# Attention sums on one core: accumulating transfers for every second tile, visits two stretches behind the scores

## The reference, cut to what matters

```python
q, k, v = x @ wq, x @ wk, x @ wv          # 32, 8 and 8 heads of 32
scores = einsum('bihd,bjhd->bhij', q, k) * 32 ** -0.5   # causal
attn = softmax(scores, axis=-1)
out = einsum('bhij,bjhd->bihd', attn, v).reshape(b, s, 1024) @ wo
```

## Time and profile before

| | us |
|---|---|
| median of 3 runs (3458.98 to 3460.59) | 3460.47 |
| the profiled execution | 3461.34 |
| its span in the trace | 3459.6 |
| PE busy | 3405.6 (98%) |
| POOL busy | 1747.4 (51%) |
| DVE busy | 2002.3 (58%) |
| ACT busy | 1467.6 (42%) |

### The profile page before, as it was taken

The page is one execution under the profiler, slowest core; times in us unless marked ns, Lnnn a source line. Parts: engine busy times, 40 slices in busy tenths (PEclk is TensorE's granted clock), DMA queues, the critical chain, the costliest instruction groups (busy, mean ns, idle before and its releaser), DMA issues.

```text
span 3459.6 us, 61790 instructions
## 1 busy us (share of the span) xinstructions
PE 3405.6 (98%) x25202; PEld 2389.0 (69%) x25202; DVE 2002.3 (58%) x3617; ACT 1467.6 (42%) x1830; POOL 1747.4 (51%) x749
## 2 busy tenths in 40 slices
PE   8999999999999999999999999999999999999998
PEld 7888886565665665666666566556558888878887
DVE  3122116777677677677777767767746766642222
ACT  3111112555665565565565556556553223211111
POOL 0000003888988998898898898889540000000000
PEclk9999999999999999999999999999999999999999
DMA  6334344021111111211112111110037777655553
GB/s 217 112 125 124 114 135 97 22 55 50 32 46 50 38 38 50 51 30 48 50 33 53 50 35 43 50 40 10 26 113 239 232 234 229 220 203 167 170 174 132
DMA packets 248556, 340.60 MB, mean 98 GB/s; under 512 B 55648, under 2 KB 150368, under 8 KB 248288
## 3 DMA queue, kind: packets, MB, share of 16 engines
q1 hardware_dynamic: 248288, 336.87, 32.6%
HBM read 203.08 MB, written 133.17 MB: 97 GB/s over the span
## 4 chain that ended last, share of the span: by engine, by line
PE 77%; POOL 18%; ACT 2%; DVE 2%; issue 1%; DMA 0%; POOLq 0%; ACTq 0%; SPq 0%; DVEq 0%
POOL p_psums L694 16%; PE p_acc L42 13%; PE p_o L771 12%; PE p_acc L44 12%; PE p_acc L43 12%; PE p_qm L722 11%; PE p_km L764 8%; PE p_km L757 2%; DVE p_part_max L883 1%; POOL p_psums L690 1%; ACT p_probs L847 1%; PE p_ag_ps L1198 1%; PE p_qm L726 1%; PE p_km L759 1%; PE p_acc L1187 1%
## 5 line engine op out<-in xcount | busy, mean ns | idle before, releaser
L883 DVE TENSOR_REDUCE p_part_max<-p_qm 128x1 f32<-128x512 f32 (+3 forms) x2240 | 1400.7, 672 | 556.0 <-PE p_qm L722 348.4
L694 POOL TENSOR_TENSOR p_psums<-p_psums,p_probs 128x1024 f32<-128x1024 f32 x620 | 1480.3, 2388 | 92.5 <-ACT p_probs L847 2.9
L847 ACT ACTIVATE p_probs<-p_km 128x1024 f32<-128x1024 f32 x896 | 887.6, 1023 | 463.1 <-PE p_km L764 451.7
L722 PE MATMUL p_qm<-p_k_st,p_q_st 96*128 96x512 f32 (+3 forms) x2560 | 907.8, 415 | 10.3 <-ACT p_neg_max L829 4.5
L722 PEld LDWEIGHTS p_qm<-p_k_st,p_q_st 96*128 96x128 f32 x2560 | 473.9, 191 | 255.7 <-issue 93.2
L764 PE MATMUL p_km<-p_q_st,p_k_st 97*128 97x512 f32 x1792 | 602.8, 418 | 12.6 <-ACT p_probs L847 8.3
L771 PE MATMUL p_o<-p_probs,p_v 128*32 128x256 f32 (+1 forms) x9216 | 566.6, 372 | 0.0
L771 PEld LDWEIGHTS p_o<-p_probs,p_v 128*32 128x32 f32 x9216 | 271.1, 110 | 222.1 <-issue 52.3
L764 PEld LDWEIGHTS p_km<-p_q_st,p_k_st 97*128 97x128 f32 x1792 | 311.3, 192 | 101.2 <-ACT p_probs L847 59.9
L690 POOL TENSOR_TENSOR p_psums<-p_probs 128x1024 f32<-128x1024 f32 x110 | 261.9, 2381 | 189.2 <-ACT p_probs L847 189.2
L679 POOL MEMSET p_k_st<- 1x2048 f32 x2 | 3.6, 1805 | 511.6 <-PE p_acc L44 511.6
(11 more groups left out here) (153 smaller groups left out, 3980.9 us busy)
## 6 DMA issues: line engine op xcount, KB each, us to landing
p_q_st<-q_hi SPq DMA_DIRECT2D x128, 256.0 KB, 4.7
p_x_raw<-in_xT SPq DMA_DIRECT2D x64, 256.0 KB, 3.5
q_hi<-p_out_hi SPq DMA_DIRECT2D x64, 256.0 KB, 2.0
q_lo<-p_out_lo SPq DMA_DIRECT2D x64, 256.0 KB, 2.4
p_q_st<-q_lo SPq DMA_DIRECT2D x64, 256.0 KB, 4.4
attended_T<-p_o_raw SPq DMA_DIRECT2D x128, 128.0 KB
p_a_raw<-attended_T SPq DMA_DIRECT2D x32, 512.0 KB, 9.7
p_recip<-reciprocals SPq DMA_DIRECT2D x128, 128.0 KB, 6.9
```

Of the source, the lines that this page charges most:

```text
L694: pool.tensor_tensor(sums[:, :, :], sums[:, :, :], probs[(n * NS + s) % PB][:, :, :], ALU.add).then_inc(added, 1)
L722: last = pe.matmul(bank[:, x * keys:(x + 1) * keys], q_st[par][0:ROWS, c, h + x, sub * P:(sub + 1) * P], k_st[par][0:ROWS, j * CK:j * CK + ...
L847: act.activation(tile[:, :, :].rearrange("p h q -> p (h q)"), km[s % 2][:, :, :].rearrange("p a b -> p (a b)"), ACT.Exp, scale=SCALE).then ...
L883: dve.reduce_max(part_max[c][:, h:h + heads, sub, j], qm[bank_of(i)][:, 0:item_width(i)].rearrange("p (h k) -> p h k", h=heads), AX.X).the ...
```

## The change

The plan now gives each chunk a written order of work for its sums. Chunks 4 to 7 have a chain of tiles 4, 6, 8, 10 (2, 3, 4 and 4 of them) that POOL doesn't add itself. SP copies the first of the chain (tile 4) to a new buffer `fsums` (512 KB; there is one), and POOL then issues, for each further tile of the chain, a transfer inside SBUF that adds the tile to `fsums` (`accum_op`). Each of these waits for the landing of the one before. At the end of the chunk POOL waits for the last landing and adds `fsums` to its own sum. The plan:

| chunk | 0 | 1 | 2 | 3 | 4 | 5 | 6 | 7 | all |
|---|---|---|---|---|---|---|---|---|---|
| tiles | 2 | 4 | 6 | 8 | 10 | 12 | 14 | 16 | 72 |
| to POOL before | 0 | 3 | 5 | 6 | 8 | 9 | 11 | 12 | 54 |
| to POOL after | 0 | 3 | 5 | 6 | 7 | 7 | 8 | 10 | 46 |
| to the transfers after | 0 | 0 | 0 | 0 | 2 | 3 | 4 | 4 | 13 |
| adds of POOL before | 0 | 2 | 4 | 5 | 7 | 8 | 10 | 11 | 47 |
| adds of POOL after (the combining one counted) | 0 | 2 | 4 | 5 | 7 | 7 | 8 | 10 | 43 |

POOL's order in chunk 7, for example, is: adds of tiles 1, 2, 3, 5, transfer of 6, add of 7, transfer of 8, add of 9, transfer of 10, adds of 11, 12, 13, the combining add. The last group has its plan of before. The ring has 21 tiles instead of 22 (`fsums` takes the place of one). PE visits a stretch two stretches behind its scores instead of one (`LAG`), so the last two stretches of a group are visited in the next group, and stores and the load of v move with them. The diff, cut to its core:

```diff
-    PB = 22
+    PB = 21
+    LAG = 2
...
-    POOLED = [0, 3, 5, 6, 8, 9, 11, 12]
-    SUMS = Sums(POOLED)
-    LAST_SUMS = Sums([c + 1 if c > 2 else 0 for c in range(NC)])
+    def order(fetched, added):
+        if not added:
+            return []
+        chain = [4 + 2 * x for x in range(fetched)]
+        tiles = [t for t in range(NT) if t not in chain][:added]
+        steps = []
+        for t in sorted(chain + tiles):
+            if t in chain:
+                steps.append(("fetch" if t > chain[0] else "copy", t))
+            else:
+                steps.append(("add" if steps else "first", t))
+        if fetched:
+            steps.append(("fetched", 0))
+        return steps
+    SUMS = Sums([order(*counts) for counts in ((0, 0), (0, 3), (0, 5), (0, 6), (2, 7), (3, 7), (4, 8), (4, 10))])
+    LAST_SUMS = Sums([order(0, c + 1 if c > 2 else 0) for c in range(NC)])
...
+        fsums = sb("p2_fsums", [P, REP, CQ], F32)
...
+            def begin_fetched(n, c):
+                earlier = [e for e in range(c) if SUMS.copied_before[e + 1] > SUMS.copied_before[e]]
+                if earlier:
+                    sp.wait_ge(added, n * NADD + SUMS.adds_through_fetched(earlier[-1]))
+                elif n > 0:
+                    sp.wait_ge(added, (n - 1) * NADD + SUMS.adds_through_fetched(NC - 1))
+                begin = n * NS + FIRST_STEP[c] + 4
+                sp.wait_ge(exp_done, begin + 1)
+                sp.dma_start(fsums[:, :, :], probs[begin % PB][:, :, :]).then_inc(copied, 16)
...
+                if not last:
+                    for c in range(NC):
+                        if SUMS.copied_before[c + 1] > SUMS.copied_before[c]:
+                            events.append((FIRST_STEP[c] + 5.6, "begin fetched", c))
...
+                        elif what == "fetch":
+                            pool.wait_ge(exp_done, n * NS + s + 1)
+                            pool.wait_ge(copied, 16 * copies)
+                            at_least(pool, fetched, 16 * landed)
+                            pool.dma_start(fsums[:, :, :], tile[:, :, :], accum_op=ALU.add).then_inc(fetched, 16)
+                            landed += 1
+                        elif what == "fetched":
+                            pool.wait_ge(fetched, 16 * landed)
+                            pool.wait_ge(added, adds)
+                            pool.tensor_tensor(sums[:, :, :], sums[:, :, :], fsums[:, :, :], ALU.add).then_inc(added, 1)
+                            adds += 1
...
-                    if not plan.on_pool(s):
+                    if plan.on_pe(s):
                         last = weighted(ones[:, :], probs[(n * NS + s) % PB], CQ, offset(s), False)
...
-                    if sl > 0:
-                        values(n, par, sl - 1, plan)
+                    if sl >= LAG:
+                        values(n, par, sl - LAG, plan)
                     elif n > 0:
-                        values(n - 1, 1 - par, NSL - 1, SUMS)
+                        values(n - 1, 1 - par, NSL + sl - LAG, SUMS)
...
-            values(NG - 1, 1, NSL - 1, LAST_SUMS)
+            for sl in range(NSL - LAG, NSL):
+                values(NG - 1, 1, sl, LAST_SUMS)
...
-                if plan.on_pool(u % NS):
+                if plan.copied_through(u % NS):
+                    at_least(act, copied, 16 * ((n if u >= 0 else n - 1) * NCOPY + plan.copied_through(u % NS)))
+                elif plan.fetched_through(u % NS):
+                    at_least(act, fetched, 16 * ((n if u >= 0 else n - 1) * NFETCH + plan.fetched_through(u % NS)))
+                elif not plan.on_pe(u % NS):
                     at_least(act, added, (n if u >= 0 else n - 1) * NADD + plan.adds_through(u % NS))
```

More of the change, by code:

```diff
@@ L391, in attend, with __init__ @@
     class Sums:
[L393 to L398, removed]
+        def __init__(self, orders):
+            self.orders = orders
+            counted = lambda kinds: [sum(what in kinds for order in orders[:c] for what, _ in order) for c in range(NC + 1)]
+            self.adds_before, self.copied_before, self.fetched_before = (
+                counted(("add", "fetched")), counted(("copy",)), counted(("fetch",)))
+            self.chunks = [sum(bool(order) for order in orders[:c]) for c in range(NC + 1)]
@@ L399, in on_pool, with on_pe, first_pair @@
+        def on_pe(self, s):
             c, t = STEPS[s]
-            return t < self.pooled[c]
+            return (t not in self.first_pair(c) and ("add", t) not in self.orders[c]
+                    and not any(what in ("copy", "fetch") and tile == t for what, tile in self.orders[c]))
+        def first_pair(self, c):
+            return [tile for what, tile in self.orders[c] if what == "first"]
         def adds_through(self, s):
             c, t = STEPS[s]
-            return self.adds_before[c] + max(1, t)
@@ L406, in attend, with fetched_through @@
-    POOLED = [0, 3, 5, 6, 8, 9, 11, 12]
-    SUMS = Sums(POOLED)
-    LAST_SUMS = Sums([c + 1 if c > 2 else 0 for c in range(NC)])
-    NADD, NCHUNK = SUMS.adds_before[NC], SUMS.chunks[NC]
+            at = self.orders[c].index(("first", t) if t in self.first_pair(c) else ("add", t))
+            return self.adds_before[c] + max(1, sum(what in ("add", "fetched") for what, _ in self.orders[c][:at + 1]))
+        def fetched_through(self, s):
+            c, t = STEPS[s]
+            order = [tile for what, tile in self.orders[c] if what == "fetch"]
+            return self.fetched_before[c] + order.index(t) + 1 if t in order else 0
@@ L684, in group @@
                     sums = psums[c % 2]
[L685 removed]
+                    adds, landed = n * NADD + plan.adds_before[c], n * NFETCH + plan.fetched_before[c]
+                    copies = n * NCOPY + plan.copied_before[c]
+                    for what, t in plan.orders[c]:
                         s = FIRST_STEP[c] + t
[L687 to L688 removed]
+                        tile = probs[(n * NS + s) % PB]
+                        if what == "copy":
+                            copies += 1
+                        elif what == "first":
+                            first = tile
+                        elif what == "fetch":
[9 more added lines that the diff above has]
+                            adds += 1
+                        elif first is not None:
+                            pool.wait_ge(exp_done, n * NS + s + 1)
@@ L697, in gpsimd @@
+                            first = None
+                            adds += 1
+                        else:
+                            pool.wait_ge(exp_done, n * NS + s + 1)
+                            pool.wait_ge(added, adds)
+                            pool.tensor_tensor(sums[:, :, :], sums[:, :, :], tile[:, :, :], ALU.add).then_inc(added, 1)
+                            adds += 1
             group(0, SUMS)
```

36 lines of the change are left out of this document (22 added, 14 removed).

## The result

The change makes the kernel slower: 3578.97 us (median of 4 runs, 3573.87 to 3582.03) against 3460.38 (4 runs) on the same chip, a ratio of 1.0346 [1.0334, 1.0358], +118.6 us. The prediction was 3420, its range 3412 to 3530: the time moved the other way and lies outside the range. The profiled execution took 3582.03 us, a span of 3580.2.

What follows compares the result with a forecast made beforehand. PE was taken to set the pace (busy 123.31 of a steady group's 124.44 us), with POOL near it. Fewer sets on PE (-32.3) and vanished waits (-9.3) made -41.6, from 3461.34 to 3420 us; range 3412 to 3530.

Steps and rivals of the forecast that it cites:

- 2.15 us a group for five sets: On PE, five fewer sets of `ones` matmuls at 0.43 us each; over 15 groups -32.3 us.
- -9.3 for the later visits: PE's weight loads no longer wait for chunk 7's sums at group ends, 14 waits in all: -9.3 us.
- The sum of -41.6: Whole kernel: -32.3 from PE's sets and -9.3 from its waits, giving 3419.7, stated as 3420.
- the free 13.7 us: POOL, chunks 4 to 7: transfers may cost it 13.7 us a group before PE has to wait for chunk 7's sums.
- rival (1): POOL becomes the bound, waiting for landings before the next transfer or combining add: slower, 3540 or 3530; chance 0.36.
- L: Time from an accumulating transfer's issue on POOL to its landing: taken as 4.0 us, between 2.6 and 5.4.
- X: POOL's time to issue one accumulating transfer: taken as 1.0 us, between 0.43 and 2.38.
- S: POOL's wait for a landing beyond one add of cover, L - X - 2.51: 0.5 us, on 7 of 9 transfers.
- the bounds worked out from loads (5.4): Upper end for the landing of an accumulating 512 KB transfer, by the loads' slope: 1.8 + 3.6 = 5.4 us.
- Leaves the transfer engines to it: Reason for the middle landing time of 4.0 us: a steady group moves only 44 GB/s, so transfer engines are free.
- The estimate of 4.1 us: Landing of an accumulating transfer if adding halves the rate, with 2.0 us fixed; would leave nearly nothing free.
- an estimate of 3.2 us: Landing of 512 KB issued from GpSimd: about 2.0 us plus bytes at 436 GB/s; would keep the full gain.

Runs made afterwards that it cites:

- e13: The change with transfers at every third tile, two each in chunks 5, 6 and 7, at least two adds behind each, 59 tiles off PE: 3417.31 us, ratio 0.9877.
- e1: The change with the plan of sums of before (no transfers, 47 adds a group), later visits and ring of 21 kept: 3449.07 us, ratio 0.9973.
- e8: The change with only 4 transfers a group, at every third tile, beside 36 adds from chunk 4 to 7; 58 tiles off PE: 3427.63 us, ratio 0.9907.
- e4: The change with the loads of q and k for later groups cut to 16 of 512 columns, transfers kept: 3521.02 us (one run).
- e10: The change with its nine accumulating transfers a group made plain copies of the same 512 KB: 3427.04 us, ratio 0.9914.
- e5: Later visits, plan of sums of before, no transfers, but six idle adds on POOL ahead of chunk 7's last add: 3563.36 us, ratio 1.0302.
- e2: The change with each accumulating transfer cut to 128 of 1024 columns (64 KB instead of 512): 3421.6 us, ratio 0.9895.
- e15: The change with each accumulating transfer cut to two of four heads (256 KB): 3432.16 us, ratio 0.9920.
- e3: The change with transfers at every third tile instead of every second, two adds behind each, loads whole: 3439.53 us, ratio 0.9943.
- e6: Later visits, plan of sums of before, no transfers, but four idle adds on POOL ahead of chunk 7's last add: 3487.42 us, ratio 1.0080.
- e9: The change with visits one stretch behind the scores again (LAG 1), transfers, plan of sums and ring of 21 kept: 3683.33 us (one run).

## Why the prediction was wrong

**Right: the gain.** 2.15 us a group for five sets: e13 has 121.69 where e1, with the plan of before, has 123.80, 2.11 less. -9.3 for the later visits: -9.6. The sum of -41.6: e13, with the same tiles taken off PE, has -42.0. The ring of 21 and SP's new waits cost nothing that e1 or e13 shows, and the plain copy lands after 3.0 us, inside its bounds.

**Right: the free 13.7 us.** e8, with 94.1 us of POOL work from chunk 4 to 7, has no wait of PE over 0.9 us, and the excess of the change over 13.7 (9.4) is close to its wait (8.8). The place was named too, in rival (1), at a chance of 0.36: the wait of the next transfer and of the combining add for the landing before.

**Wrong: L, the time to land**, "4.0, the middle". The cost of the nine transfers was put at 12.5 us and is 23.1. By the rows:
- X: 0.61 us from the issue to the start of the next add, and that add lasts 2.67 instead of 2.38. That makes 0.9 where 1.0 was taken, and gives back 9 x 0.1 = 0.9 us.
- L beside the cut loads: 4.6 (e4) for 4.0. With the smaller X, S grows by 0.7, on 7 transfers 4.9 us. Beside the whole loads the seven landings that POOL waited for in the group shown took 4.5 to 6.8 us, 5.3 on the mean, near the end of the bounds worked out from loads (5.4). The reason given against that end, that the transfer engines are free in this stage, does not touch the price, since the adding itself takes them for twice as long (e10).
- From a landing to the next issue POOL takes another 0.6 us: 5.1 to 5.3 us from issue to issue at a landing of 4.6 (e4). S had no such term; five transfers follow a transfer, 3.0 us.
- Collision: the two waits of chunk 7 took 6.23 and 7.41 us from issue to issue instead of some 5.2, together 3.2 us. "Leaves the transfer engines to it" read the mean of a group, 44 GB/s. The loads are bunched: SP issued six from 1755.82 to 1759.66, between chunk 7's first transfer (1754.42) and its second (1760.65).

-0.9 + 4.9 + 3.0 + 3.2 = 10.2 of the 10.6 us that were missing. e4 shows how far this holds, by the first add of its chunk 4 and the last of its chunk 7 in one group:

```profile
1642.80 2.38 POOL L767 TENSOR_TENSOR p_psums<-p_probs 128x1024 f32<-128x1024 f32 x1
...
1739.57 2.34 POOL L762 TENSOR_TENSOR p_psums<-p_psums,p_fsums 128x1024 f32<-128x1024 f32 x1
```

From 1642.80 to 1741.91 are 99.1 us, so with the loads cut the transfers cost 18.8, 6.3 over the forecast, where the first three terms make 7.0. The whole loads add 103.4 - 99.1 = 4.3, of which the two waits are 3.2.

Beside the rows, the two rules of the Trainium skill come apart. By its page "Collectives: The Full Stack" (The bandwidth ceiling) an add inside a transfer runs at half the rate; the queue's rows agree (twice the engine time for the same bytes). The estimate of 4.1 us that rests on it was the better one, and still under the 4.6 measured. The formula of the Trainium skill's page "DMA: Bandwidth & Descriptors" (Anatomy of one DMA - SWDGE path), an estimate of 3.2 us, fits the plain copy that lands after 3.0 us, and no adding one of 512 KB.

**Why worse than rival (1)'s own 3540.** It priced POOL's lateness alone. By its rule the measured 23.1 would give 3420 + 14 x 9.4 = 3552, already over the range's top of 3530, and 27 us less than was measured. The steady groups show what it lacked: e13 to the kernel after, 121.69 to 133.92, are 12.23 us, of which PE's idle time is 9.50 - 0.75 = 8.75 and its slower matmuls 124.42 - 120.94 = 3.48. Over the whole kernel PE is busy for 47 us more than in e13 (3365.2), with the same 24602 matmuls. That term, a clock that falls in the wait that the change makes, was in neither the sum nor a rival. The wait in e5 that lasted 5.44 us cost 2.3 beyond its length, and this one of 8.80 cost 3.48; that the greater length makes the difference is likely but not shown.

## What to carry to other kernels

A transfer that adds is not a copy: take its price from an adding transfer of that size, at the place where it will run, and give it as many adds of cover as its landing beside the loads needs (here two, and four in chunk 7), not one. When an engine sits near the bound, ask what each us past its slack costs at the other end: here 1.3 to 1.5 us of time for each us of wait. And an instruction removed from a chain that is itself the cover of a wait frees nothing.

## What the runs showed of the hardware

- Accumulating from SBUF to SBUF lands, by medians, after 2.6 us for 64 KB (e2), 3.4 for 256 KB (e15) and 4.6 for 512 KB (e4; 4.9 in the change, up to 9.1 in e3); the plain one of 512 KB after 3.0 from either queue (e10). For the same bytes it holds the transfer engines twice as long (10.7% of the change's span, 5.6% of e10's).
- To issue one costs POOL 0.9 us (plain: 0.6), a part of it as a longer add behind it (2.67 for 2.38 us).
- The collision goes both ways: the 8 KB of maxima land after 3.8 us beside whole loads and adding transfers, after 1.8 beside the loads without transfers (before), and after 1.9 beside adding transfers with the loads cut (e4).
- PE's clock was at its lower level after a wait of 5.44 or 8.80 us, in two cases of 14 after one of at most 2.6 us (e6), and after one of 1.82 us in e9; with PE at work it came back some 6 to 10 us later.
- An add of a tile to itself takes POOL 1.96 us, of two tiles 2.38.
